# An attention stage whose values, projections and transposes run one pair of steps later, with the value projections moved to the first iteration of a batch and part of the layer norm on GpSimd

## The reference

```python
h = concatenate([tok(...), txt], axis=1)         # (8, 768, 256), float32
xn = (h - mean) / sqrt(var + 1e-5)
q = rope(xn @ Wq)     # 16 heads of 64
k = rope(xn @ Wk)     # 4 key heads of 64
v = xn @ Wv           # 4 value heads of 64
attn = softmax(q k^T * 64**-0.5)                 # 4 query heads share a key head
h = h + (attn @ v) @ Wo
h = h + experts(layernorm(h))                    # 8 experts, the best 2 of each token
```

## Time and profile before

| | |
|---|---|
| median of three runs | 2489.94 us (2486.7 to 2493.41) |
| profiled execution, its own time | 2496.86 us |
| its span | 2495.1 us |
| attention stage, in that span | about 125 to 1712 us |
| busy, whole span | PE 84%, DVE 71%, ACT 43%, POOL 36% |
| granted TensorE clock, attention from 500 to 1500 us | 0.99 of full speed |

### The profile page before, as it was taken

How to read it: one execution, slowest core, us unless ns; L and a number is a source line. 1 busy time by engine, 2 the same in 40 slices (tenths; PEclk the granted TensorE clock), 3 DMA queues, 4 the chain that set the end, 5 groups by cost and what they waited for, 6 DMA issues and landing times. The chain is left out here.

```text
span 2495.1 us, 60022 instructions
## 1 busy us (share of the span) xinstructions
PE 2106.5 (84%) x21124; PEld 1267.3 (51%) x21125; DVE 1781.0 (71%) x3303; ACT 1074.6 (43%) x2468; POOL 892.0 (36%) x781
## 2 busy tenths in 40 slices
PE   0446999999999999999999999975989839999990
PEld 0432444444444444444444444433777639999980
DVE  8429999999999998998998998991334334444440
ACT  2014555655555655555555565550111114444430
POOL 1043245245345244344344442401133334444441
PEclk6579999999999999999999999997888769999995
DMA  4122333433433433333333333324766448998978
GB/s 147 36 70 60 89 81 97 106 81 97 107 80 97 105 83 96 100 85 97 97 87 90 88 91 87 86 76 141 219 213 198 150 154 207 213 215 210 211 171 204
DMA packets 242808, 307.00 MB, mean 123 GB/s; under 512 B 61600, under 2 KB 186016, under 8 KB 242464
## 3 DMA queue, kind: packets, MB, share of 16 engines
q1 hardware_dynamic: 208032, 252.27, 36.5%
q0 software_dynamic: 21888, 39.20, 8.1%
q10 hardware_dynamic: 12672, 12.58, 1.6%
HBM read 154.07 MB, written 80.64 MB: 94 GB/s over the span
## 5 line engine op out<-in xcount | busy, mean ns | idle before, releaser
L629 ACT ACTIVATE a_prob<-ps_s,a_nmax 128x768 f32<-128x768 f32 x768 | 686.4, 898 | 625.9 <-DVE a_nmax L748 625.9
L748 DVE TENSOR_REDUCE a_nmax<-ps_s 128x1 f32<-128x768 f32 x768 | 697.6, 949 | 102.8 <-PE ps_s L561 91.9
L754 DVE STREAM_TRANSPOSE a_probT<-a_prob 128x768 f32<-128x768 f32 x768 | 699.1, 952 | 14.4 <-ACT a_prob L629 14.4
L561 PE MATMUL ps_s<-a_kT,a_qT 64*128 64x384 f32 x3072 | 625.9, 521 | 90.5 <-ACT a_prob L629 78.1
L568 PE MATMUL ps_o<-a_probT,a_vrep 32*64 32x384 f32 x12288 | 567.6, 495 | 31.2 <-DVE a_probT L754 28.3
L561 PEld LDWEIGHTS ps_s<-a_kT,a_qT 64*128 64x128 f32 x3072 | 261.6, 188 | 432.6 <-ACT a_prob L629 292.6
L690 POOL TENSOR_TENSOR a_o<-a_o,a_invrow 128x1536 f32<-128x1536 f32 x32 | 110.5, 3455 | 880.1 <-DMA a_invrow<-inv_d 865.4
L568 PEld LDWEIGHTS ps_o<-a_probT,a_vrep 32*64 32x64 f32 x12288 | 246.1, 133 | 325.4 <-issue 139.1
L448 POOL TENSOR_TENSOR a_prod<-a_raw,a_table 128x384 f32<-128x384 f32 x312 | 303.3, 1004 | 57.0 <-ACT a_raw L621 53.4
L1282 POOL DMA_INDIRECT acc_d<-e_y,e_row_i x104 | 161.4, 1552 | 247.8 <-DVE e_y L1302 244.5
L913 PE MATMUL ps_ra<-wo,r_oT 128*128 128x256 f32 x768 | 203.9, 421 | 38.5 <-DMA r_oT<-oT_d 22.8
(11 more groups left out here) (203 smaller groups left out, 1362.0 us busy)
## 6 DMA issues: line engine op xcount, KB each, us to landing
e_w<-in_L_ffn_W_dram SPq DMA_DIRECT2D x104, 512.0 KB, 4.4
a_qT<-a_qp SPq DMA_DIRECT2D x512, 96.0 KB, 2.2
a_vrep<-a_vraw SPq DMA_DIRECT2D x512, 48.0 KB, 1.9
a_invrow<-inv_d SPq DMA_DIRECT2D x64, 384.0 KB, 5.2
oT_d<-a_o SPq DMA_DIRECT2D x32, 768.0 KB, 3.5
r_oT<-oT_d SPq DMA_DIRECT2D x192, 128.0 KB
e_x<-xs_d SPq DMA_DIRECT2D x104, 132.0 KB
acc_d<-v_zero POOLq DMA_DIRECT2D x8, 768.0 KB, 9.7
```

What stands on the lines that cost most here:

```text
L561: last = pe.matmul(S[:, s % 2, r, 0:HALF], qT[rows, par, 2 * hp + c, P * t:P * t + P], kT[rows, par, :], start=True, stop=True)
L629: act.activation(prob[:, s % RING, :].rearrange("p (r k) -> p r k", r=2), S[:, s % 2, :, 0:HALF], ACT.Exp, bias=nmax[:, s % RING:s % RING ...
L748: v.tensor_reduce(nmax[:, s % RING:s % RING + 1], S[:, s % 2, :, 0:HALF], AX.XY, ALU.max, negate=True).then_inc(max_ready, 1)
L754: v.transpose(turned(par, s), prob[:, s % RING, :]).then_inc(t_ready, 1)
```

## The change

It does six things. (1) Values, output copies, inverse and jobs of an iteration come two steps later: groups at s = 3 to 17, copies at 18 and 19, inverse at 19, jobs at 19, 21, 23 and "25", which is step 1 of the next iteration. (2) VectorE no longer does four transposes at the last step; the last pair's transposes come at step 1 of the next iteration. (3) The V jobs move from g = 3 of the batch before to g = 0 of the batch itself, ahead of that iteration's Q jobs, and out of the prologue; their evacuation waits for the value moves of the iteration before. (4) In SyncE's program the values of g = 0 are moved after `invrow` is read back; elsewhere the order stays: the key moves of g = 3 stand ahead of the value moves in both. (5) Of the statistics, parts 3 to 5 (three refinements) run on GpSimd for every batch but the first; the two integer operations of the guess join part 2 on VectorE, and parts 0 to 2 run at g = 2, s = 19, 21, 23. (6) GpSimd normalises at g = 1 in every batch, at the start of that iteration's work, ahead of the rotation of the queries, with the refinements just before it.

```diff
-    JOBS = [Q_JOBS, Q_JOBS + N_JOBS, Q_JOBS + K_JOBS, Q_JOBS + V_JOBS]
-    FIRST = N_JOBS + K_JOBS + Q_JOBS + V_JOBS + Q_JOBS
+    JOBS = [V_JOBS + Q_JOBS, Q_JOBS + N_JOBS, Q_JOBS + K_JOBS, Q_JOBS]
+    Q_AT = [len(V_JOBS), 0, 0, 0]
+    FIRST = N_JOBS + K_JOBS + Q_JOBS + Q_JOBS
-    JOB_AT = {0: [], 4: [17, 21, 23, 23], 7: [17, 19, 19, 21, 21, 23, 23], 8: [17, 17, 19, 19, 21, 21, 23, 23]}
+    JOB_AT = {0: [], 4: [19, 21, 23, 25], 7: [19, 19, 21, 21, 23, 23, 25], 8: [19, 19, 21, 21, 23, 23, 25, 25]}
-    GROUP_AT = {2 * n + 1: n for n in range(NJ // GROUP)}
-    TURN_AT = {s: [s - 3, s - 2] for s in range(3, STEPS, 2)}
-    TURN_AT[STEPS - 1] += [STEPS - 2, STEPS - 1]
-    O_AT = {16: (0, 1), 17: (2, 3)}
-    INV_AT = 17
-    STATS_AT = [(KV - 2, 17), (KV - 2, 19), (KV - 2, 21), (KV - 1, 17), (KV - 1, 19), (KV - 1, 21)]
-    STATS_1_AT = [(0, 17), (0, 17), (0, 19), (0, 19), (0, 21), (0, 21)]
+    GROUP_AT = {2 * n + 3: n for n in range(NJ // GROUP)}
+    O_AT = {18: (0, 1), 19: (2, 3)}
+    INV_AT = 19
+    STATS_AT = [(KV - 2, 19), (KV - 2, 21), (KV - 2, 23)]
+    STATS_1_AT = [(0, 17), (0, 19), (0, 21)]
...
             def _(sp):
                 def move_v(b, g):
                     pause(sp, pv_done, (b * KV + g) * NJ)
-                    hold(sp, x_out, FIRST_AT["q1"] if b == 0 else job_no(b, 0, 0))
+                    hold(sp, x_out, job_no(b, 0, len(V_JOBS)))
...
                     if not last_it(i):
                         move_q((g + 1) % 2, i + 1)
-                        if g == KV - 1:
-                            hold(sp, part["k"], b * (2 * LINKS) + 4 * LINKS)
-                            move_k(0, 0)
-                    move_v(b, g)
+                    if g == KV - 1 and not last_it(i):
+                        hold(sp, part["k"], b * (2 * LINKS) + 4 * LINKS)
+                        move_k(0, 0)
+                    if g > 0:
+                        move_v(b, g)
                     if not first_it(i):
                         move_inv(i - 1)
+                    if g == 0:
+                        move_v(b, g)
+                    if not first_it(i):
                         store(i - 1)
...
             def _(act):
-                        if (job, c) == ("v", 0):
-                            free = v_in, i * (V_MOVES * 16) + V_MOVES * 16
+                        if (job, c) == ("v", 0) and bb:
+                            free = v_in, i * (V_MOVES * 16)
...
             def _(pool):
                 def normalise(n):
+                    if n > 0:
+                        for at in range(3, 6):
+                            stats(pool, n, at)
                     hold(pool, norm_dve, n * NORMS + NORMS)
...
                 def iteration(b, g):
                     i = b * KV + g
+                    if not last_batch(b) and g == 1:
+                        normalise(b + 1)
                     if not last_it(i):
                         for c in range(2):
                             rotate(pool, "q", c, ...)
                     if g == KV - 1 and not last_batch(b):
                         for c in range(2):
                             rotate(pool, "k", c, ...)
-                    if not last_batch(b) and g == (0 if b else 1):
-                        normalise(b + 1)
                     if not first_it(i):
                         scale_o(i - 1)
...
             def _(v):
                         maxima(i, s)
-                        for n in TURN_AT.get(s, ()):
-                            turn(i, par, n)
+                        if s % 2 and s > 1:
+                            for n in (s - 3, s - 2):
+                                turn(i, par, n)
+                        elif s % 2 and not first_it(i):
+                            for n in (STEPS - 2, STEPS - 1):
+                                turn(i - 1, 1 - par, n)
```

## The result

The changed kernel takes 2510.35 us (median of 5 runs, 2506.32 to 2512.71); the kernel before, beside it, 2493.06 us (5 runs). The ratio is 1.0057, with an interval of 1.0041 to 1.0073: slower by 0.6%. The profiled execution took 2512.71 us, its span 2511.0. The forecast was 2491 us, with "the same" as the likeliest sign; slower had 32%. All ratios are of executions in the chip's faster state, which leaves out one execution of before (2696.06 us) and one of the four of `e6_both` (5415.64 us).

The account below looks back on a forecast made before the run. A closed ring of SyncE and GpSimd waits was taken as the bound. Start +0.7, six batches at +0.9 and end -5.3 us summed to +0.8 us, so 2491 us for the median; range 2482 to 2515 (8 in 10).

Parts of the forecast that it names:

- the other three turns unchanged: Times between successive sets of query moves, other than from g=0 to g=1: claimed to stay as before.
- `inv_d` = 3.05: SyncE's link from writing the inverse to DRAM to reading it back (the trip): 3.05 us of a 46.06 us sum.
- The ring: SyncE waits for GpSimd and GpSimd for SyncE, a closed loop of 46.06 us an iteration, claimed to set the pace.
- turn from g=0: Time from the query moves of g=0 to those of g=1: claimed 46.8 us, +0.9 us a batch.
- The end: Last batch, from its g=0 query moves (T0) to the drain: 157.4 us claimed against 162.7, a gain of 5.3.
- R: Time of the refinement's 12 dependent GpSimd operations, ahead of the query rotation at g=1: taken as 3.5 us.
- rival B: Slower, because small dependent operations on GpSimd are dear: 2518 us, or 2539 at the bound; chance 23%.
- Rule against row: Compared the skill's GpSimd and VectorE rules with trace rows; by the rule, refinement 4.9 us and sum +9 us.
- The tie at the inverse: At g=0 the inverse is made 10.9 us after the query moves, SyncE's queue arrives at 11.3; counted as nothing.
- rival C: Slower at g=0: value moves beside `invrow`'s transfer, or the inverse comes late; 2 to 3 us a batch, 2506; chance 9%.
- Rival D: Faster: the SyncE-GpSimd loop isn't closed and the main chain's 8 us a batch come through, 2437 us; chance 9%.
- a floor that the prediction had already worked out: Value moves of g=1 wait for the running values, until 56.5 us after the query moves of g=0.

Follow-up runs that it names:

- e6_both: Kernel after, with GpSimd scaling the output of iteration i - 2 behind the rotation, SyncE's store moved with it, refinements and normalisation behind the rotation; ratio to before 0.9869.
- f1_pad32: Kernel after with 32 small multiplications at the head of TensorE's attention block, changing no result; 2487.25 us, ratio to the kernel before 0.9967.
- e5: Kernel before, with GpSimd scaling the output of iteration i - 2 behind the rotation and SyncE storing it behind the query moves; ratio 1.0055.
- f2: Kernel after with the inverse write issued ahead of the value moves at g=1 to 3, the read left behind them; ratio to the kernel before 1.0257.
- f3: e6_both with the inverse's write and read at g=0 taken apart and the value moves between them; ratio to the kernel before 0.9891.

## Why the prediction came out as it did

**The time was in the range, the sign was the second choice.** 2510 lies in 2482 to 2515. The kernel came out slower for a reason that none of the rivals names, so that the range held it is luck.

**The step that failed:** "Where g is 1, 2 or 3 its links keep their order", from which I took "the other three turns unchanged". The order was kept, and the trip in it was not: 4.6 us at g=1 and 4.4 at g=3, for 3.4 and 3.0. In the sum it is the term `inv_d` = 3.05, used for all four trips; it should have been 12.7 a batch plus about 1.5 for each hit (two a batch), here 15.6. The same collision makes most of the start: the value moves of iteration 1 came 1.3 us late (265.23 for 263.96; forecast 0.7), and then the first trip took 5.01 us for 3.00, the third 4.72 for 3.06; batch 1 was 4.6 us late where I said 0.7. With the padding all of this goes: those value moves start at 262.85, and batch 1 at 394.44, before at 394.46. Why the value moves, which no trip precedes, move with the padding too, was not traced.

**The ring stands.** f1_pad32 is the change as it was predicted, with the trips as the prediction took them. Its turn from g=0 grows by 46.64 - 45.88 = 0.8 us, forecast 0.9. Its other turns are 46.4, 46.1 and 49.4, forecast unchanged from 46.3, 46.4 and 49.9; part of the 0.7 won there is before's own four hits. Its period is +0.1 (forecast +0.9).

**The end.** Its drain starts at T0 + 156.4 (1681.95 - 1525.56; T0 is here that of batch 7), forecast 157.4, before 162.7. In the kernel after it starts at T0 + 159.4 (1704.73 - 1545.33), 2.0 later than forecast, with no packet in the trips of that batch; what holds it was not traced. In all the padded kernel is 7.6 us faster than before, where the sum said 0.8 slower. So the sum was right to about 8 us without the hits, which cost about 23 (2510.35 - 2487.25, on different chips; by ratios, 1.0057 for 0.9967, 0.9%). Without them the verdict sits on the bound between the same and faster.

**R** was taken at 3.5 and measured 3.5 us. So rival B, with 23% the largest, fell: the refinement costs what the fit to GpSimd's rows gave. The Trainium skill, GPSIMD Engine Reference, Key points, has elementwise work on VectorE about twice as fast; here the operation takes 0.20 us at a pitch of 0.28 where VectorE has 0.17 at 0.2. At this size the trace doesn't agree with a factor of two. Two slips stand in "Rule against row": 12 x 0.4 is 4.8, not 4.9, and the row of 0.96 us is an operation with one input, so it can't bear out a rule on two. The trace does so one line further: at 226.95 and 228.85 us, beside the same rotation, operations with two inputs took 0.91 and 0.92 us.

**The signs that I named.** ScalarE's wait is gone. VectorE's 1.44 us at the hand-over are gone at two of four; where the first group waits, VectorE still stands 1.5 to 1.8 us, about 5 us later, and it stands twice a batch, 1.1 us each, where the value projections lie. The first group waits twice a batch, 44.1 / 6 = 7.4 us a batch, 3.7 each time, for the "5 us at g=0 and 3 at g=1". The tie at the inverse held: one wait of 0.7 us; and the turn from g=0 is 46.2, so the 2 to 3 us that rival C put there are not there. That its 2506 us lies near 2510 is chance. Rival D fell: the batch took no less. e5 and e6 add that the ring isn't the only loop: cut alone it gives nothing, cut with this change 1.3%.

**When a packet lengthens a trip.** Twelve of the traces (all but f2 and f3) hold 372 trips. In 210 of them no packet of q8, and none of a second instruction queue, q14, with packets of 8 KB, starts near the write: none of these takes over 3.4 us. In 106 a packet of q8 alone starts between 0.35 us before the write and 2.85 behind it: all but one take over 3.4 us, 3.5 to 4.3 where it starts within 0.35 us before, 4.2 to 5.1 where it starts 1.8 to 2.6 behind. Six packets that start 2.9 to 3.1 us behind lengthen nothing (3.04). So a "hit" by the window of 3.1 us misses a few: the kernel after has three trips of 3.5 to 4.0 us at g=2 that it doesn't count, and their packets start 0.0 to 0.3 us before the write. A packet of q14 alone adds less: 32 trips, 3.26 us in the mean, 8 of them over 3.4.

**Still open:** why the packet lengthens the trip. In the trace of after such a packet takes 0.9 to 1.5 us, and the four writes are waited for together; that the packet holds up one of them on a DMA engine fits the times above, but no run varied that. And the 0.4 us a batch by which the period's +2.6 misses the trips' +2.9 was not traced.

## What to carry to other kernels

Once two queues form a closed ring, the shortest link in it deserves a look: here the wait for a small DMA to land was on the path in full, and a packet of instructions in it cost 1.0 to 1.5 us each time, in every batch again where the phase repeated. Before believing in a difference of under 1%, shift the program's instructions by a few dozen real ones in an idle stretch and time it again: here that moved the same kernel by 0.9% (0.7% between two paddings on one chip), more than the change did. And before moving work off a ring, compute the next loop that closes: two of my experiments lost to a floor that the prediction had already worked out, and a third to a loop that I had not looked for.

## What the hardware showed that I had not expected

The DMA view names an instruction queue (q8, 143 packets and 2.34 MB in the span of after); single packets of it, 16 KB each, stand beside trips of 4.6 instead of 3.1 us, and padding TensorE's program moves them. The same kernel before took 2454.14 us on one chip and 2493 to 2498 us on others, 1.6 to 1.8% apart; the ratio of the kernel after to it, taken twice, each time beside it on one chip, stayed within 0.1% (1.0057 and 1.0049).
